# Attention scores from split q and k in fp32r passes for three heads of four, mask and row scales made by VectorE

## The reference, cut to what matters

```python
q = rope(rmsnorm(x @ Wq.T)); k = rope(rmsnorm(x @ Wk.T)); v = x @ Wv.T
k_all = concat([k_cache[block_table], k]);  v_all = concat([v_cache[block_table], v])
valid = (arange(512) < cache_seqlens[b]) for the cached columns, True for the new ones
scores = where(valid, (q @ k_all.T) / sqrt(128), -1e30)
o = softmax(scores) @ v_all;   x = x + s4_convolution(o @ Wo.T)
x = x + ffn(lora(x))          # linear layers with a LoRA, then a gated one
```

## Time and profile before

| what | value |
|---|---|
| median of 3 runs | 1350.19 us (1349.44 to 1350.74) |
| profiled execution | 1351.09 us |
| its span, first to last instruction | 1349.4 us |
| mean granted TensorE clock | 0.98 of full speed |
| TensorE busy | 1276.0 us |
| VectorE, ScalarE, GpSimd busy | 783.2, 657.8, 563.1 us |
| attention, both halves | about 183 to 507 us and about 860 to 1184 us of the span |
| HBM traffic | 203.33 MB read, 10.49 MB written |

### The profile page before, as it was taken

One profiled execution on the slowest core, in us unless ns is written; L12 is line 12 of the kernel. 1 busy time (PEld: TensorE's weight loads), 2 busy tenths in 40 slices (PEclk: granted clock), 3 DMA queues, 4 the chain that ended last, 5 costly groups with the idle time before them and its releaser, 6 DMA issues.

```text
span 1349.4 us, 26762 instructions
## 1 busy us (share of the span) xinstructions
PE 1276.0 (95%) x6994; PEld 1038.0 (77%) x6994; DVE 783.2 (58%) x1657; ACT 657.8 (49%) x1934; POOL 563.1 (42%) x805
## 2 busy tenths in 40 slices
PE   6899979999999998998989999799999999999998
PEld 4678858888888886765657788588888888878756
DVE  5976546666666666852147766466666666655412
ACT  3676645555555554331235766455555555554320
POOL 3344335455445534533033444354554554454320
PEclk9999979999999998998989999899999999999999
DMA  6231387887888825305033323888878888334300
GB/s 238 86 134 62 122 233 224 233 239 221 228 220 225 230 70 177 129 1 187 33 111 125 121 83 105 237 226 229 243 215 230 223 220 229 86 108 146 106 0 32
DMA packets 148102, 214.80 MB, mean 159 GB/s; under 512 B 25844, under 2 KB 120374, under 8 KB 142006
## 3 DMA queue, kind: packets, MB, share of 16 engines
q1 hardware_dynamic: 128646, 202.75, 51.6%
q10 hardware_dynamic: 18576, 9.05, 2.5%
q0 software_dynamic: 800, 2.10, 0.6%
HBM read 203.33 MB, written 10.49 MB: 158 GB/s over the span
## 4 chain that ended last, share of the span: by engine, by line
PE 81%; DVE 7%; issue 4%; DMA 3%; ACT 3%; ACTq 2%; POOL 1%; SPq 0%; DVEq 0%; POOLq 0%; PEldq 0%
PE PS L985 17%; PE PS L938 9%; PE PS L953 8%; PE PS L943 8%; PE PS L900 4%; PE PS L896 4%; PE PS L892 4%; PE PS L994 4%; PE PS L1044 3%; PE PS L1035 3%; PE PS L1041 3%; PE PS L1093 2%; PE PS L871 2%; ACTq L655 2%; PE PS L1072 2%
## 5 line engine op out<-in xcount | busy, mean ns | idle before, releaser
L985 PE MATMUL PS<-probT,kv 128*128 128x128 f32 x2048 | 270.4, 275 | 0.0
L985 PEld LDWEIGHTS PS<-probT,kv 128*128 128x128 f32 x2048 | 248.8, 192 | 0.1
L516 POOL TENSOR_TENSOR ring_parts<-ring,kv_parts 128x512 fp32r<-128x512 f32 x96 | 128.6, 1345 | 233.2 <-ACT kv_parts L638 233.2
L779 ACT ACTIVATE ring<-ring,smin 128x544 f32<-128x544 f32 x192 | 143.6, 748 | 141.4 <-DVE smin L1401 141.4
L1401 DVE CUSTOM_DVE_ANT_0 ring<-PS,mask,rq 128x544 f32<-128x544 f32 x192 | 150.5, 784 | 79.7 <-PE PS L943 77.6
L1407 DVE COPY probT<-PS 128x512 f32<-128x512 f32 x256 | 175.6, 686 | 3.8 <-PE PS L953 3.8
L938 PE MATMUL PS<-kv,q_now 128*128 128x288 f32 x512 | 169.9, 414 | 2.9 <-ACT q_now L754 2.9
L943 PE MATMUL PS<-kv,q_now 128*128 128x256 f32 x512 | 154.8, 384 | 0.0
L892 PE MATMUL PS<-kv_parts 128*128 128x512 f32 x384 | 115.0, 418 | 19.2 <-ACT kv_parts L638 15.8
L551 POOL TENSOR_SCALAR ring<-ring,rinv 128x512 f32<-128x512 f32 x192 | 132.8, 692 | 0.0
L602 POOL TENSOR_TENSOR ring_parts<-ring,kv_parts 128x512 fp32r<-128x512 f32 x64 | 89.6, 1405 | 102.7 <-ACT kv_parts L814 102.6
(11 more groups left out here) (196 smaller groups left out, 2176.4 us busy)
## 6 DMA issues: line engine op xcount, KB each, us to landing
kv<-in_kpages SPq DMA_DIRECT2D x512, 128.0 KB, 2.3
kv<-in_vpages SPq DMA_DIRECT2D x496, 128.0 KB, 3.2
ring<-in_w SPq DMA_DIRECT2D x46, 1024.0 KB, 4.9
kv<-in_xT SPq DMA_DIRECT2D x4, 1024.0 KB, 9.0
v_new<-kv ACTq DMA_DIRECT2D x64, 64.0 KB, 2.3
k_new<-kv ACTq DMA_DIRECT2D x16, 256.0 KB, 2.3
kv<-k_new SPq DMA_DIRECT2D x32, 128.0 KB, 2.6
kv<-v_new SPq DMA_DIRECT2D x32, 128.0 KB, 2.1
```

The costliest lines, as they stand in the source:

```text
L779: nc.scalar.activation(a, a, ACT.Exp, scale=-1.0, bias=smin[:, g:g + 1], accum_out=rsum[:, g:g + 1]).then_inc(exp_done, 1)
L985: mm = nc.tensor.matmul(PS[:, at:at + D], vbuf(bpar)[:, c, gg * D:(gg + 1) * D], probT[:, g % 2, c * P:(c + 1) * P], start=(c == 0 and a = ...
```

## The change

In heads 0, 1, 2 and 4, 5, 6 of a batch the scores are no longer one plain fp32 product. q and k are each split into an fp32r upper part and an fp32r lower part, and three products are summed in PSUM: upper q by upper k, upper q by lower k, lower q by upper k, each in two matmuls of 288 and 256 columns. Heads 3 and 7 stay plain fp32. ScalarE makes the upper k (544 columns a head, two steps ahead, after the scores of the running step) and the upper q of three heads; GpSimd makes the lower k, in place in the key buffer, ahead of the scaling of the probabilities in its list; VectorE makes the lower q in step 1 and 5. GpSimd no longer makes mask and row scales: VectorE does both at the end of step 3, with a mask formula of another form (the column number and the length, both multiplied by 2 to the 100th, subtracted and cut at 0). The wait for the key pages moves from TensorE to ScalarE (for split heads), and the copy of q no longer waits for the scores. Below, lines that only count a wait as past, and most of the removed lines, are left out.

```diff
-        q_now = sb("q_now", [P, 2, GU * D])
+        q_hi = sb("q_hi", [P, 2, NS * D], F32R)      # NS = 3 heads of a unit
+        q_lo = sb("q_lo", [P, 2, NS * D], F32R)
+        q_now = sb("q_now", [P, 2, D])
+        k_hi = sb("k_hi", [P, 2, LK], F32R)
...
 GpSimd
-                def mask_of(b, par):
-                    nc.gpsimd.tensor_copy(rq[:, par, :], rowscale[:, ds(b * HK, HK)]).then_inc(mask_ready, 1)
-                    nc.gpsimd.tensor_copy(len_now[:, par:par + 1], lens_b[:, ds(h * HB + b, 1)]).then_inc(mask_ready, 1)
-                    pool.wait_ge(mask_ready, 3 * (h * HB + b) + 2)
-                    nc.gpsimd.tensor_scalar(mask[:, par, 0:LC], con("iota"), len_now[:, par:par + 1], BIG,
-                                            ALU.is_ge, ALU.mult).then_inc(mask_ready, 1)
+                def lower_keys(b, par, first, last=False):
                     for g in range(HK):
                         s = h * STEPS + b * HK + g
+                        if g % GU < NS:
+                            e = g // GU * NS + g % GU
+                            pool.wait_ge(khi_ready, (h * HB + b) * NSB + e + 1)
+                            nc.gpsimd.tensor_tensor(
+                                kbuf_lo(par)[:, :, g, :], kbuf(par)[:, :, g, :],
+                                k_hi[:, e % 2, :].rearrange("p (j t) -> p j t", t=PSIZE), ALU.subtract)\
+                                .then_inc(klo_ready, 1)
                         if g >= 2:
                             scale_probs(b, g - 2, first)
                         elif not first:
                             scale_probs(b - 1, g - 2 + HK)
...
 ScalarE
-                    nc.scalar.activation(q_now[:, u, :], qo[:, at], ACT.Copy).then_inc(q_copied, 1)
+                def upper_q(u, at):
+                    nc.scalar.activation(q_hi[:, u, :], qo[:, ds(at, NS * D)], ACT.Copy).then_inc(qhi_ready, 1)
+                    nc.scalar.activation(q_now[:, u, :], qo[:, ds(at + NS * D, D)], ACT.Copy).then_inc(q_copied, 1)
+                def upper_keys(b, par, g):
+                    if g == 0:
+                        act.wait_ge(k_in[par], h * (136 * HB) + (b - par) * 136 + 272)
+                    e = g // GU * NS + g % GU
+                    nc.scalar.activation(k_hi[:, e % 2, :].rearrange("p (j t) -> p j t", t=PSIZE),
+                                         kbuf(par)[:, :, g, :], ACT.Copy).then_inc(khi_ready, 1)
...
+                    if (g + 2) % GU < NS and not (last and g + 2 >= HK):
+                        act.wait_ge(s_ready, s + 1)
+                        if g + 2 < HK:
+                            upper_keys(b, par, g + 2)
+                        else:
+                            upper_keys(b + 1, 1 - par, g + 2 - HK)
                     if g < HK:
                         act.wait_ge(masked, s + 1)
...
 TensorE
+                    if a == 0:
+                        pe.wait_ge(qlo_ready, h * (QUADS + 1) + b * UNITS + u + 1)
+                    pe.wait_ge(khi_ready, (h * HB + b) * NSB + e + 1)
+                    mm = nc.tensor.matmul(PS[:, at:at + mid], q_hi[:, u, q], hi[:, 0:mid], start=True, stop=False)
+                    nc.tensor.matmul(PS[:, at + mid:at + LK], q_hi[:, u, q], hi[:, mid:LK], start=True, stop=False)
+                    pe.wait_ge(klo_ready, (h * HB + b) * NSB + e + 1)
+                    nc.tensor.matmul(PS[:, at:at + mid], q_hi[:, u, q], lo[:, 0:SPLIT, g, :],
+                                     start=False, stop=False)
+                    nc.tensor.matmul(PS[:, at + mid:at + LK], q_hi[:, u, q], lo[:, SPLIT:NPP + 1, g, :],
+                                     start=False, stop=False)
+                    nc.tensor.matmul(PS[:, at:at + mid], q_lo[:, u, q], hi[:, 0:mid], start=False, stop=True)
+                    nc.tensor.matmul(PS[:, at + mid:at + LK], q_lo[:, u, q], hi[:, mid:LK],
+                                     start=False, stop=True).then_inc(s_ready, 1)
...
 VectorE
+                def lower_q(u, at):
+                    V.tensor_tensor(q_lo[:, u, :], qo[:, at], q_hi[:, u, :], ALU.subtract).then_inc(qlo_ready, 1)
+                def mask_of(b, par):
+                    V.tensor_scalar(mask[:, par, 0:LC], con("iota"), lens_b[:, ds(h * HB + b, 1)], 0.0,
+                                    ALU.add, ALU.max).then_inc(mask_ready, 1)
+                    V.tensor_copy(rq[:, par, :], rowscale[:, ds(b * HK, HK)]).then_inc(mask_ready, 1)
...
                         V.reciprocal(rinv[:, g:g + 1], rsum[:, g:g + 1]).then_inc(rinv_ready, 1)
+                        if g % GU == 1:
+                            nb, u = (b, 1) if g == 1 else ((b + 1) % HB, 0)
+                            dve.wait_ge(qhi_ready, h * (QUADS + 1) + b * UNITS + g // GU + 2)
+                            lower_q(u, ds(nb * (HQ * SEQ) + u * GU * D, NS * D))
+                        if g == 3:
+                            if not first:
+                                dve.wait_ge(masked, s - g)
+                            mask_of((b + 1) % HB, 1 - par)
```

More of the change, by code:

```diff
@@ L29 @@
 UNITS = HK // GU
+NS = GU - 1
+NSB = UNITS * NS
 SLOTS = 4
@@ L43 @@
 QUADS = STEPS // GU
-BIG = 1e30
+BIG = 2.0 ** 100
 MAGIC = 12582912.0
@@ L79, in constants @@
     put("ident", np.eye(P))
-    put("iota", np.arange(LC)[None, :])
+    put("iota", BIG * np.arange(LC)[None, :])
     power = (10000.0 ** (np.arange(0, D, 2) / D)).astype(np.float32)
@@ L145, in build @@
         rq = sb("rq", [P, 2, HK])
-        len_now = sb("len_now", [P, 2])
         smin = sb("smin", [P, 8])
@@ L316, in build @@
         v_free = sem("v_free")
+        qhi_ready = sem("qhi_ready")
         q_copied = sem("q_copied")
+        qlo_ready = sem("qlo_ready")
+        khi_ready = sem("khi_ready")
+        klo_ready = sem("klo_ready")
         s_ready = sem("s_ready")
@@ L569, in scale_batch @@
                             scale_probs(b - 1, g - 2 + HK)
[L570 to L575, removed]
                 pool.wait_ge(table_in, 16 * h + 32)
@@ L772, in keep_o, with step @@
                         .then_inc(ot_read, 1)
-                def step(b, g, first):
+                def step(b, par, g, first, last=False):
                     s = h * STEPS + b * HK + g
+                    if (g + 2) % GU < NS and not (last and g + 2 >= HK):
[4 more added lines that the diff above has]
+                            upper_keys(b + 1, 1 - par, g + 2 - HK)
                     if g < HK:
@@ L792, in _ @@
                 act.wait_ge(turn_read, NQK * (h + 1))
-                copy_q(0, slice(0, GU * D))
+                upper_q(0, 0)
+                upper_keys(0, 0, 0)
+                upper_keys(0, 0, 1)
                 for g in range(HK):
-                    step(0, g, True)
+                    step(0, 0, g, True)
                 with act.Fori(0, HB // 2 - 1) as bb:
@@ L798, in _ @@
                         for g in range(HK):
-                            step(bb * 2 + 1 + n, g, False)
+                            step(bb * 2 + 1 + n, 1 - n, g, False)
                 for g in range(HK):
-                    step(HB - 1, g, False)
+                    step(HB - 1, 1, g, False, True)
                 spread_new(HB - 1, 1)
@@ L926, in scores @@
                     u, a = g // GU, g % GU
[L927 to L930, removed]
+                    at = 1024 * (g % 2) + 512 - SPLIT * PSIZE
+                    mid = SPLIT * PSIZE
+                    raw = kbuf(par)
                     if not (first and g < 2):
                         pe.wait_ge(masked, s - 1)
-                    at = 1024 * (g % 2) + 512 - SPLIT * PSIZE
@@ L935, in scores @@
-                    mid = SPLIT * PSIZE
+                    if a == NS:
+                        pe.wait_ge(q_copied, h * (QUADS + 1) + b * UNITS + u + 1)
+                        pe.wait_ge(k_in[par], h * (136 * HB) + (b - par) * 136 + 272)
+                        nc.tensor.matmul(PS[:, at:at + mid], q_now[:, u, :], raw[:, 0:SPLIT, g, :],
+                                         start=True, stop=True)
+                        nc.tensor.matmul(PS[:, at + mid:at + LK], q_now[:, u, :], raw[:, SPLIT:NPP + 1, g, :],
+                                         start=True, stop=True).then_inc(s_ready, 1)
+                        return
@@ L936, in scores @@
+                    if a == 0:
+                        pe.wait_ge(qlo_ready, h * (QUADS + 1) + b * UNITS + u + 1)
+                    e = u * NS + a
+                    pe.wait_ge(khi_ready, (h * HB + b) * NSB + e + 1)
+                    hi, lo = k_hi[:, e % 2, :], kbuf_lo(par)
                     q = slice(a * D, (a + 1) * D)
-                    mm = nc.tensor.matmul(PS[:, at:at + mid], q_now[:, u, q], kbuf(par)[:, 0:SPLIT, g, :],
-                                          start=True, stop=True)
+                    mm = nc.tensor.matmul(PS[:, at:at + mid], q_hi[:, u, q], hi[:, 0:mid], start=True, stop=False)
@@ L1163, in prologue @@
                 link(V.tensor_copy(lens_b[:, :], lens_bi[:, :]))
```

(1 more changed line is left out.)

29 lines of the change are left out of this document (13 added, 16 removed).

## The result

The changed kernel takes 1330.99 us (median of 4 runs, 1330.55 to 1331.59) beside 1350.47 before: a ratio of 0.9853, 95% interval 0.9838 to 0.9869. The prediction said 1353, with more chance for slower than for faster; the measured time lies inside its range of 1330 to 1384 by 1 us only. The change made the kernel 19.5 us faster.

What follows compares the result with a forecast made beforehand. TensorE was taken to bound attention, with two cycles across engines close behind. Stalls would eat the matmul saving, so 1351.1 + 0 + 3 = 1354, or 1353 as a median; range 1330 to 1384.

Steps and rivals of the forecast that it cites:

- the two cycles: Across engines: step loop, minimum to minimum, 1.95 us; bank cycle, transposes not before the previous slot's minimum plus 1.55.
- the mask held until 0.30 after the subtraction: VectorE, end of step 3: a mask meeting GpSimd's running subtraction ends 0.30 us after it, taking over 1 us.
- the walk: One batch followed slot by slot through the engines' lists, giving 19.92 us against 19.93 before, without reserve.
- the saving of 1.14 is eaten by three stalls: TensorE, per batch: the gain from cheaper split scores is lost to waits at transposes, leaving 19.92 us against 19.93.
- 0.27 + 0.48 + 0.37 = 1.12: TensorE's forecast waits in us for VectorE's copy, at the transposes of slots 3, 5 and 7 of a batch.
- caught behind the next GpSimd instruction once more, about 0.40: VectorE, end of step 3: the small row-scale copy after the mask is held up again, making step 4's minimum late.
- ScalarE's 2.20 in step 0 and 4: Exponential's start to the end of line 771, with two q copies: 2.20 us, more than a slot of 2.06.
- Behind the lower q 0.72 from R to the next minimum: VectorE, steps 1 and 5: from reciprocal's end (R1 5.20, R5 15.45) past lower q to next minimum (5.92, 16.17).
- The starts: First scores of each half wait for upper k, a subtraction and two hand-overs: about +1.5 us, +3 for both.
- the mask is not held up: Rival: mask and row scales cost 0.6 us, step 4's minimum is on time, 19.44 a batch, 1337; chance 0.20.
- Everything hides: Rival: VectorE's slack absorbs the extra work, -36 + 3 us, 1317; chance 0.10.
- three holes of TensorE: Sign: TensorE waits for VectorE's copy at transposes of slots 3, 5 and 7, 1.1 us a batch; otherwise forecast wrong.

Runs made afterwards that it cites:

- e7: The changed kernel without the third product (lower q by upper k left out of the scores, lower q still made): 1320.41 us, 0.9770 of the kernel before.
- e1: The changed kernel with VectorE computing only 8 of the 512 mask columns: 1331.88 us, 0.9852 of the kernel before.
- e2: The changed kernel with the copy of the row scales placed ahead of the mask: 1331.21 us, 0.9848 of the kernel before.
- e3: The changed kernel with the mask computed a second time once a batch, into a spare tile: 1339.59 us, 0.9916 of the kernel before.
- e5: The changed kernel with mask and row scales back on GpSimd at their old place: 1372.31 us, 1.0148 of the kernel before.
- e4: The changed kernel with VectorE's lower q moved ahead of its wait for the exponential, before the reciprocal: 1327.18 us, 0.9825 of the kernel before.

## Why the prediction was wrong

**What held.** That TensorE bounds the stage and what its slots cost; the two cycles (1.54 and 1.98 in e7, 1.55 and 1.95 in the text); the mask held until 0.30 after the subtraction (0.29, though for 0.92 on the mean and not for over 1 us); the lower q at 0.56; upper k 0.657 for 0.65, lower k 1.347 for 1.35; GpSimd's scalings and the key pages in time; the first scores of each half, 1.5 later (3.0 for both).

**What failed** is the walk, and with it "the saving of 1.14 is eaten by three stalls". It set 0.27 + 0.48 + 0.37 = 1.12; the changed kernel has 0.11 at slot 3 and nothing at slots 5 and 7. Three terms made it, all of them too dear, in a walk that said of itself it had no reserve:

- *The `rq` copy "caught behind the next GpSimd instruction once more, about 0.40"*: it took 0.16 in 32 of 34 places, most of it beside its neighbours (it starts 0.08 before the mask's record ends, and the minimum 0.03 before its own does), and GpSimd's small scaling waited in its place (0.46 for 0.29). From the minimum of step 3 to that of step 4 the walk had 11.38 - 7.89 = 3.49; measured 2.93 (404.75, 407.68). Of these 0.56 less, 0.24 are the copy's length, 0.20 the overlaps on either side of it, and 0.12 a subtraction that came earlier. The scores of step 4 were there at just that time, so the stall of 0.48 vanished whole. e1 shows that the mask's length is free, e2 that 0.13 more is too, and e3 that 0.36 more costs 0.2.
- *ScalarE's 2.20 in step 0 and 4*: the two q copies were priced with 0.11 each beyond their columns; the second starts 0.41 after the first and the whole is 2.08 (exponential 398.93, next one 401.01). The exponentials of step 1 and 5, set 0.15 late, were on time.
- *Behind the lower q 0.72 from R to the next minimum*: the minimum starts 0.08 before the lower q's record ends. In steps 5 to 6 it is 0.62; in steps 1 to 2, where VectorE idles 0.24 ahead of the lower q ("issue" in the profile, which names no cause) instead of 0.15, it is 0.71, and only there was a stall left.

Against these the matmuls cost 0.03 more a split head than taken (0.75 for 0.72), 0.18 a batch. Put into the same walk, the measured terms (0.75, 2.08, 1.98 and 1.54 for the cycles, 0.71 and 0.62 behind the lower q, 2.93 over the mask) leave a stall of less than 0.1 at slot 3, none at slot 5 and none at slot 7, where the spare time is only 0.03: an estimate worked out from these rows, which agrees with what the trace has. As a sum, 18.79 + 0.18 + 0.11 = 19.08, measured 19.11, where the text had 19.92: 32 x 0.81 = 26 us between them, more than the whole error of 22.

**What the sum left out** is the table load. The starts were put at +3, which is what the first scores cost; the load behind ScalarE's copy added 0.94 a half, 1.9 in all, the other way.

The rivals: "the mask is not held up" came out nearest in time (1337) but by another mechanism, it is held up and costs nothing. "Everything hides" (1317) priced the split scores and starts too low; its claim about VectorE's slack was nearly true. By the prediction's own signs of being wrong, two of its three holes of TensorE are missing.

## What to carry to other kernels

A walk along the engines' lists finds the places where engines meet. Every place that this one named turned up, all three in e7 and one of them in the changed kernel. But where it finds several small stalls in a row without reserve, their sum is no surer than the errors of its terms taken together, and so is the sign of the forecast. Check the hand-over terms first (how far a record's end overlaps its successor, what the second of two held-up instructions costs), then the instruction lengths. Look also at what an engine does only once at the start of a stage: an instruction put ahead of it can move it onto the path (the table load, 0.94 a half). An engine 58% busy can still refuse one piece of 2.4 us (e5), and one at 64% can take a held-up instruction for nothing if a slot's slack lies there (e1). When a change moves work to an engine with a waiting gap in each step, put it into the gap (e4).

## What the runs showed of the hardware

- At a granted clock of 1.00 (2.4 GHz) fp32r matmuls of 288 and 256 columns start 0.13 and 0.12 apart, those of 512 columns 0.227: one column a cycle, and about 0.013 each beside it.
- ScalarE's table load takes 1.28. It was free (183.41) until a copy that waits for the first scores stood ahead of it (188.12); then 0.94 of it lay between the first minimum and its exponential, in both halves.
- Where VectorE and GpSimd contend, either of them can be the one that waits. VectorE's mask and its 8-column copy wait out a running subtraction (0.92 and 0.73). What comes right behind them fares differently from run to run: in the batches of the changed kernel the second instruction takes 0.16 and GpSimd's scaling grows, 0.46 for 0.29; in e2 the second loses 0.12 to 0.18; in e1 it takes 0.35 instead of 0.16 to 0.19 in 7 of 34 places. Beside the lower q GpSimd's scaling grows too, 0.67 for 0.29 (402.25 to 402.92; the lower q ends at 402.85). In the stretch at 16 to 23 us of the kernel before, where GpSimd had nothing but subtractions, five such VectorE instructions, one after another, took 1.0 to 1.7 each, some of them of 8 columns only. And at the start of each half of the changed kernel the order is the other one: the mask goes through in 0.36 and the copy behind it is held until the subtraction ends, 1.28:

```profile
184.54 0.36 DVE L1434 TENSOR_SCALAR mask<-consts,lens_b 128x512 f32<-128x512 f32 x1
184.82 1.28 DVE L1436 COPY rq<-rowscale 128x8 f32<-128x8 f32 x1
...
184.42 2.94 POOL L574 TENSOR_TENSOR kv_parts<-kv,k_hi 128x544 fp32r<-128x544 f32 x2 [13.72 <-ACT k_hi L765]
```

The first of these two subtractions takes 1.65 instead of 1.35. So 0.16 is what the batches of this kernel show, not a rule for the second instruction; what decides it stays open. The Trainium skill ("SBUF — State Buffer", section "Who interferes with whom") says that whichever starts first keeps the port and the other blocks for all of it. That either engine can be the one that blocks was seen here. Who started first can't be read from the records: the scaling of 402.25 began 0.04 before the lower q and the subtraction of 184.42 began 0.12 before the mask, and both times it was GpSimd's instruction that grew.
